# Context attention of four decoder layers: ScalarE empties three of the four turned banks of a round, VectorE one

## The reference, cut to what matters

```python
q = (x @ Wq)  -> 8 heads of 64, times 64 ** -0.5, rotary on the first 32 of each head
k = (ctx @ Wk), v = (ctx @ Wv)      # 154 rows, 8 heads of 64; rotary on k
sim = einsum('bhid,bhjd->bhij', q, k)          # 512 x 154 for each head
a = softmax(sim)
out = einsum('bhij,bhjd->bhid', a, v)          # 512 x 64 for each head
x = x + out.reshape(512, 512) @ Wo + bo
```

## Time and profile before

| | |
|---|---|
| median of 3 runs | 4059.58 us |
| the profiled execution's own time | 4062.76 us |
| its span (first to last instruction) | 4061.1 us |
| granted TensorE clock, mean | 0.973 of full speed |
| PE busy | 3737.5 us, 92% of the span |
| DVE busy | 2716.3 us, 67% |
| ACT busy | 1981.0 us, 49% |
| POOL busy | 1016.3 us, 25% |

### The profile page before, as it was taken

How to read it: one execution, slowest core, us unless ns; L and a number is a source line. 1 busy time by engine, 2 the same in 40 slices (tenths; PEclk the granted TensorE clock), 3 DMA queues, 4 the chain that set the end, 5 groups by cost and what they waited for, 6 DMA issues and landing times. The chain is left out here.

```text
span 4061.1 us, 70254 instructions
## 1 busy us (share of the span) xinstructions
PE 3737.5 (92%) x22984; PEld 2305.7 (57%) x22984; DVE 2716.3 (67%) x8004; ACT 1981.0 (49%) x5746; POOL 1016.3 (25%) x1109
## 2 busy tenths in 40 slices
PE   6999899999999998999879998999999999989997
PEld 4645446556565664566546444455655656645665
DVE  3787767777767745775347877677777677457663
ACT  1732345555555532675327224455555555317653
POOL 0154323332323201101201553233223232010012
PEclk8999999999999999999979999999999999999998
DMA  2100000000000011010110000000000100200101
GB/s 78 43 18 1 1 24 18 24 18 24 1 35 8 2 51 55 2 69 25 53 40 22 17 1 7 18 18 24 18 24 1 38 4 2 76 30 2 69 24 56
DMA packets 37447, 105.83 MB, mean 26 GB/s; under 512 B 3552, under 2 KB 28640, under 8 KB 33632
## 3 DMA queue, kind: packets, MB, share of 16 engines
q1 hardware_dynamic: 35040, 97.11, 6.8%
q0 software_dynamic: 2048, 4.20, 0.3%
HBM read 92.25 MB, written 9.04 MB: 25 GB/s over the span
## 5 line engine op out<-in xcount | busy, mean ns | idle before, releaser
L625 PE MATMUL ps_O<-wide,V 128*64 128x256 f32 (+4 forms) x5152 | 597.8, 394 | 1.8 <-ACT wide L653 1.8
L708 ACT ACTIVATE EX<-NB,neg 128x154 f32<-128x154 f32 (+3 forms) x768 | 402.6, 530 | 114.9 <-DVE neg L736 114.9
L671 POOL COPY RX<-recips 128x256 f32<-128x256 f32 (+2 forms) x356 | 157.5, 442 | 1113.4 <-DVE recips L751 1109.1
L576 PE MATMUL ps_S<-KT,QT 64*128 64x154 f32 (+7 forms) x1936 | 375.8, 458 | 60.0 <-POOL QT L1637 25.4
L762 DVE TENSOR_TENSOR QT<-ps_O,RS 128x512 f32<-128x512 f32 x212 | 146.6, 691 | 390.3 <-PE ps_O L625 389.7
L655 DVE COPY wide<-ps_P 128x512 f32<-128x512 f32 (+4 forms) x528 | 339.9, 647 | 73.2 <-PE ps_P L607 70.2
L625 PEld LDWEIGHTS ps_O<-wide,V 128*64 128x64 f32 (+4 forms) x5152 | 267.4, 127 | 195.0 <-issue 111.6
L576 PE MATMUL ps_T<-KT,QT 64*128 64x154 f32 (+5 forms) x968 | 323.9, 437 | 3.5 <-ACT EX L708 3.5
L576 PE MATMUL ps_OUT<-KT,QT 64*128 64x154 f32 (+5 forms) x968 | 326.9, 436 | 0.1
L607 PE MATMUL ps_P<-consts,EX 128*128 128x128 f32 (+1 forms) x1956 | 293.2, 286 | 25.1 <-ACT RS L662 11.7
L708 ACT ACTIVATE QT<-NB,neg 128x512 f32<-128x512 f32 (+2 forms) x512 | 311.9, 619 | 0.0
(11 more groups left out here) (460 smaller groups left out, 8011.6 us busy)
## 6 DMA issues: line engine op xcount, KB each, us to landing
weights<-in_w_dram SPq DMA_DIRECT2D x10, 1664.0 KB, 6.7
weights<-in_w_dram SPq DMA_DIRECT2D x2, 6148.0 KB, 17.2
weights<-in_w5next_dram SPq DMA_DIRECT2D x6, 1664.0 KB, 7.1
weights<-in_w_dram SPq DMA_DIRECT2D x2, 4200.0 KB, 12.4
weights<-in_reltab_dram SPq DMA_DIRECT2D x2, 4096.0 KB, 13.6
weights<-in_w_dram SPq DMA_DIRECT2D x8, 640.0 KB, 3.9
weights<-in_w_dram SPq DMA_DIRECT2D x5, 832.0 KB, 4.5
weights<-in_w_dram SPq DMA_DIRECT2D x2, 2050.0 KB, 7.6
```

Of the source, the lines that this page charges most:

```text
L576: ins = pe.matmul(S4[k][:, a * N:(a + 1) * N], QT[strip, c, qts[a] * P:(qts[a] + 1) * P], self.keys(c)[strip, 0:N], start=True, stop=True)
L625: ins = pe.matmul(O1[self.slot * j:self.slot * (j + 1), q0 * P:(q0 + self.nq) * P], self.value(c * self.hpc + j, kc), self.probs(rd, j)[:, ...
L671: pool.tensor_copy(RX[:, q0 * P:(q0 + self.nq) * P].rearrange("p (n s) -> p n s", s=self.slot), of.unsqueeze(2).broadcast_to([P, self.nq * ...
L708: ins = act.activation(ex[:, a * N:(a + 1) * N], src, ACT.Exp, bias=neg[:, at:at + 1], scale=-1.0 if self.added else 1.0, accum_out=sums[: ...
```

## The change

Only the context attention of the layers gets another string; the self attention (the same class) keeps "ADDA", which is also the default. The two other context attentions of the program, of other classes, are untouched.

```diff
-                                     late={0: [4, 5], 1: [6, 7], 2: ["X"]} if cross else {1: [4], 2: [5, "X"], 3: [6], 4: [7]})
+                                     late={0: [4, 5], 1: [6, 7], 2: ["X"]} if cross else {1: [4], 2: [5, "X"], 3: [6], 4: [7]},
+                                     split="ADAA" if cross else "ADDA")
```

## The result

The changed kernel takes 4083.47 us (median of 5 runs, 4077.09 to 4089.52) against 4059.58 (5 runs, 4053.67 to 4065.5): +23.9 us, a ratio of 1.0059 with a 95% interval of 1.0043 to 1.0074, which is 17.5 to 30.0 us. The median lies inside the stated range of 4071 to 4085, 1.5 us under its upper end. The two differ by 26.8 us, 2.9 more than the medians.

What follows compares the result with a forecast made beforehand. PE, nearly always occupied, was taken to be started mostly by ACT's last exponentials, without slack. Ten ordinary steps at 1.28 and six cold at 0.88 made 18.1 us, added to 4059.58: 4077.7, range 4071 to 4085.

Steps and rivals of the forecast that it cites:

- 0.48 for a copy on ACT's queue: A moved turn copy costs ACT 0.48 us start to start; its 0.59 record is the upper bound.
- Iteration 1: Ordinary step: last exponentials and the turning of the reciprocals come 0.48 us later.
- Projection 7: PE's other way in, iteration 1: waits for the bank ACT now empties, +0.45 us, not added to the +0.48.
- Iteration 2: Ordinary step: first exponential +0.32 us as its DVE stall goes, then another 0.48, so reciprocals turned +0.80.
- the 1.44: Cost in us of an ordinary step if none of DVE's relief helped.
- Iteration 3 and end: Ordinary step: another 0.48 us, 1.28 in all; iteration 4's copies hidden behind some 4 us of PE work.
- Cold steps: Six of sixteen steps, first turnings partly at 1.2 GHz instead of 2.4: 0.88 us each.
- A: ACT's waits before the copies to RS absorb the copy; about the same, say +3 us, 4063; chance 0.12.
- D: All four copies count in full, iteration 4 too, DVE's relief worth nothing: 30.7 us slower, 4090; chance 0.09.
- B: DVE decides, in iteration 1; each step gains up to 0.61 us, so 4050; chance 0.05.
- C: Only the total of copying matters, cheaper engine decides: 5.2 us less, 4054; chance 0.02.
- another clock in these steps: Sign of being wrong: the clock in the sixteen context attention steps differs from before.

Runs made afterwards that it cites:

- act_extra: Kernel before with one more 77x512 copy on ACT in each of the four rounds' iterations, DVE's copies untouched: 4082.06 us, ratio 1.0073.
- all_act: Changed kernel with all four turn copies of each round on ACT ("AAAA"): 4101.9 us, ratio 1.0112 against the kernel before.
- r3_only: Changed kernel with "ADAA" in round 3 alone, "ADDA" in the other rounds: 4048.41 us, one run.
- the single rounds: Changed kernel with "ADAA" in only one of rounds 0 to 3, one run each: 4070.41, 4069.69, 4065.84 and 4048.41 us.
- dve_short: Kernel before with DVE's turn copy of position 2 cut to one element in the layers' context attention, ACT unchanged: 4060.71 us, ratio 1.0002.
- the fill: Two idle PE matmuls at the head of iteration 1 of every context attention; on the kernel before, median 6.6 us or 0.15% below it.

## Why the prediction was right, and where it was short

- *What bounds the kernel:* right. ACT's last exponentials release PE, and the wait on ACT's side is a consequence: the idle times before the copies to RS are unchanged at 1.46 and 0.98, the tie is 0.87, and act_extra alone reproduces the cost.
- *0.48 for a copy on ACT's queue, not 0.59:* right (4.37 to 4.84, and 0.47 again in all_act).
- *Iteration 1:* +0.48 forecast, 5.48 to 5.97 measured. Projection 7: +0.45 forecast, though the times given with it (3431.54 and 3431.11) make 0.43; measured 2.16 to 2.60 after the first turn copy, beside the exponentials.
- *Iteration 2:* exponential 2.0 was to start 0.32 later with DVE's stall gone, the reciprocals 0.80 later. Measured: 6.62 to 6.94 after the first copy, and 10.92 to 11.73. The numbers are right, but the reason is not: the prediction has the stall go because DVE is about 0.5 earlier. In act_extra DVE isn't earlier and the stall goes all the same (0.97), because RS 0 and what follows on ACT are 0.52 later. So the 1.44 that the prediction names for a step in which none of DVE's relief helped is too much: act_extra has 1.38, and that with a copy that costs 0.52 instead of 0.48, which over three rounds is some 0.12.
- *Iteration 3 and end:* 1.28 forecast, 1.28 measured; the moved turn copy of round 3 is free, shown by r3_only and by the unchanged 13.33 behind RS 3.
- *Cold steps:* 0.88 forecast, 0.86 measured. The time 3395.30, which the prediction has for the turning of the reciprocals in the cold step, is this row of PE before:

```profile
3395.30 0.66 PE L587 MATMUL ps_O<-consts,RX 128*128 128x128 f32 x4
```

- *Rivals:* A and D are excluded by the single rounds and all_act, B by dve_short, C by all of them. The Trainium skill, page "Perfetto Trace Analysis", section "Optimizing Scalar/DVE Operations", gives Scalar the smaller overhead on PSUM. The trace after agrees in sign (595 ns a copy on ACT, 672 on DVE). Here that decides nothing: what DVE is relieved of brings 0.02 to 0.03 us in an ordinary step (dve_short), and the 0.48 on ACT's queue count in full.
- *The sum:* short, 18.1 against 23.9. The mechanism's part is right, 18.0 in the profiled pair and 20.2 where all sixteen steps are ordinary. The term that was mis-sized is the one that I set to zero: that as many steps are cold, and as deep, and that the clock outside is the same. The prediction names another clock in these steps as a sign of being wrong, and it came: ten cold steps for six. In the profiled pair that term was 3.3 us inside the steps and 5.4 outside. It is most likely scatter and no cost of the change, since all_act, which adds twice as many copies to ACT, has neither. With the fill the medians differ by 19.0. That it was scatter in the five runs of the change too isn't shown, as one trace of them is kept; the interval of 17.5 to 30 holds 18 as well as 24. That the forecast of the median came within 5.8 us is in this part luck: the difference between two executions of one kernel is often larger.

## What to carry to other kernels

An engine that is busy half the time can still be the one that sets the pace: look at whether its idle time ends on work that had been waiting for the engine itself. Such idle time is not a reserve: here a copy moved there cost its full step of the queue (start to start, 0.48, not the 0.59 of its record) in each round but the last. When whole-run times scatter by more than the effect, cut the trace at fixed instructions and compare step by step; here that told 0.02 us where the times told 10.

## What the runs showed of the hardware

The same program took 4048.8 to 4068.9 us in 24 runs, mean granted clock and time going together: the changed kernel's five runs have 4077.1 us at 0.974, 4080.6 and 4083.5 at 0.973, 4087.5 and 4089.5 at 0.971. The dips fall at places that differ from run to run and from step to step, in instruction sequences that are the same. In the context attention, where PE was busy 2.28 of the 3.20 us after the first exponential, 1.9 us of idle matmuls took the dips behind it away in all sixteen steps of each filled kernel. Whether one matmul would do wasn't tried.
